# Whole 128-row transposes in place of two 64-row halves in a local-attention decoder

## What is computed

```
x = layernorm(x + ssm(x));  x = layernorm(x + xattn(x, ctx))
for i in range(6):
    x = attn_layer(shift_tokens(x), Wqkv[i], q_scale[i], k_scale[i], Wo[i]) + x
    x = ffn_layer(shift_tokens(x), ...) + x
# attn_layer: qkv = x @ Wqkv, 16 heads of 64; q, k l2-normalised, scaled, rotated (xpos)
#   each window of 32 queries sees the 32 keys before it and its own 32, causal
#   and no further back than 32; softmax(q k^T * 8) v, then @ Wo
# ffn_layer: layer norm, a and gate = xn @ W1 + b1, (a * gelu(gate)) @ W2 + b2
```

## Time and profile before

| what | value |
| --- | --- |
| runs | 2374.88 and 2377.05 us, median 2375.97 |
| profiled execution, span | 2376.2 us |
| PE busy | 2232.7 us (94%) |
| DVE, ACT, POOL busy | 78%, 72%, 69% |
| instructions | 69401 |
| mean granted clock of TensorE | 0.981 |

### The profile page before, as it was taken

One profiled execution on the slowest core, in us unless ns is written; L12 is line 12 of the kernel. 1 busy time (PEld: TensorE's weight loads), 2 busy tenths in 40 slices (PEclk: granted clock), 3 DMA queues, 4 the chain that ended last, 5 costly groups with the idle time before them and its releaser, 6 DMA issues. The chain is left out here.

```text
span 2376.2 us, 69401 instructions
## 1 busy us (share of the span) xinstructions
PE 2232.7 (94%) x26001; PEld 1464.0 (62%) x26001; DVE 1862.1 (78%) x2680; ACT 1703.2 (72%) x3299; POOL 1649.6 (69%) x1553
## 2 busy tenths in 40 slices
PE   5889779999799999999999999999999999999996
PEld 3555446666456666666666666666666666666664
DVE  4899957777678888888888888888888888887884
ACT  5889734544377787787787777787777777777774
POOL 4777832323478778778787787787787787787782
PEclk8999989999899999999999999999999999999997
DMA  2312210000022222222222222222222222222221
GB/s 76 111 59 68 69 51 2 1 1 1 20 63 67 56 76 66 61 71 66 64 68 66 68 65 66 72 61 67 74 58 67 78 54 67 78 53 67 78 53 52
DMA packets 103196, 140.36 MB, mean 59 GB/s; under 512 B 63072, under 2 KB 64096, under 8 KB 102752
## 3 DMA queue, kind: packets, MB, share of 16 engines
q1 hardware_dynamic: 103136, 139.57, 21.7%
HBM read 56.39 MB, written 1.31 MB: 24 GB/s over the span
## 5 line engine op out<-in xcount | busy, mean ns | idle before, releaser
L1799 PE MATMUL f_psA<-f_W,f_xT 128*128 (+1 forms) x1152 | 602.0, 632 | 20.7 <-DVE f_m L1607 12.5
L1607 DVE TENSOR_TENSOR f_m<-f_psA,f_tab 128x1024 f32<-128x1024 f32 x384 | 461.5, 1222 | 120.2 <-ACT f_sq L1468 106.1
L1357 POOL TENSOR_TENSOR f_Pr<-f_Pr,f_rden 128x384 f32<-128x384 f32 x384 | 311.5, 832 | 236.6 <-DVE f_rden L1586 236.6
L1385 POOL TENSOR_TENSOR f_qkr<-f_qkr,f_rn 128x1024 f32<-128x1024 f32 x192 | 361.5, 1904 | 0.2 <-POOL f_rn L1393 0.2
L1799 PEld LDWEIGHTS f_psA<-f_W,f_xT 128*128 128x128 f32 x1152 | 188.9, 190 | 164.5 <-issue 113.4
L1468 ACT ACTIVATE f_sq<-f_psA 128x512 f32<-128x512 f32 x384 | 228.2, 594 | 78.8 <-PE f_psA L1799 76.0
L1770 PEld LDWEIGHTS f_psO<-f_PT,f_V 96*64 96x64 f32 x6144 | 203.5, 138 | 96.4 <-issue 88.5
L1375 POOL TENSOR_TENSOR f_qkr<-f_m 128x512 f32<-128x512 f32 x192 | 244.2, 1272 | 9.1 <-DVE f_m L1607 9.1
L1376 POOL TENSOR_TENSOR f_qkr<-f_m 128x512 f32<-128x512 f32 x192 | 244.2, 1272 | 0.0
L1770 PE MATMUL f_psO<-f_PT,f_V 96*64 96x64 f32 x6144 | 231.9, 227 | 1.6 <-ACT f_PT L1443 1.5
L794 POOL TENSOR_TENSOR x_Es<-x_E 128x512 f32<-128x512 f32 x64 | 81.1, 1267 | 206.1 <-DVE x_E L899 206.1
(11 more groups left out here) (167 smaller groups left out, 4873.5 us busy)
## 6 DMA issues: line engine op xcount, KB each, us to landing
f_V<-f_Vt SPq DMA_DIRECT2D x96, 384.0 KB, 4.2
f_V<-f_Vt SPq DMA_DIRECT2D x96, 256.0 KB, 3.5
f_W<-in_f_W SPq DMA_DIRECT2D x48, 344.0 KB, 3.2
m_Cb<-m_BC_rows SPq DMA_DIRECT2D x64, 256.0 KB, 3.2
f_W<-in_f_W SPq DMA_DIRECT2D x48, 296.5 KB, 4.2
f_V<-f_Vt SPq DMA_DIRECT2D x48, 128.0 KB, 5.3
f_xsA<-xall SPq DMA_DIRECT2D x97, 32.0 KB
f_xsA<-xall SPq DMA_DIRECT2D x97, 31.8 KB
```

The costliest lines, as they stand in the source:

```text
L1357: pool.tensor_tensor(pv, pv, rv.unsqueeze(3).broadcast_to([P, 2, 2, KEYS]), ALU.mult).then_inc(Pr_ready[g][j], 1)
L1385: pool.tensor_tensor(qv, qv, rv.unsqueeze(3).broadcast_to([P, 2, GH, DH]), ALU.mult).then_inc(qkr_ready[g], 1)
L1607: dve.tensor_tensor(m12[:, j, :, half].rearrange("p m (h d) -> p m h d", d=DH), psA[n % 2][:, :].rearrange("p (h d) -> p h d", d=DH).unsqu ...
L1799: pe.matmul(psA[n % 2][:, :], xT[:, t, :], weights(i, W_QKV + n * 512, 512), start=True, stop=True).then_inc(A_full[n_fill], 1)
```

## The change

Transposes take all 128 rows with the whole identity, and the banks hold other things. For the probabilities a bank now holds four heads with both halves (heads 0 to 3 in the first, 4 to 7 in the second), so `P_full` of the first bank is raised after the fourth of eight transposes, and `times_v(g, 0)` waits for both banks. For q and k one bank holds the four blocks of q and the other those of k. The copies of ACT have the same number of elements, with other patterns. There are 8 transposes where 16 were.

```diff
-        PT = sb("f_PT", [KEYS, 2, 8, HQ])
+        PT = sb("f_PT", [KEYS, 2, 4, P])
...
-                    act.activation(PT[:, j, :, :], probs_bank(g, j)[0:KEYS, :].rearrange("p (h q) -> p h q", q=HQ), ACT.Copy).then_inc(P_free[g][j], 1)
+                    act.activation(PT[:, j, :, :], probs_bank(g, j)[0:KEYS, :].rearrange("p (h q) -> p h q", q=P), ACT.Copy).then_inc(P_free[g][j], 1)
...
-                    g, half = n // 2, n % 2
+                    g, a = n // 2, n % 2
                     act.wait_ge(A_full[4 + n], v + 1)
-                    src = psA[g] if half else psP
-                    a = WIN + half * HQ
-                    act.activation(qkT[:, q, :, 4 * g:4 * g + 4, a:a + HQ], src[:, :].rearrange("p (a c q) -> p a c q", a=2, c=4), ACT.Copy).then_inc(A_free[4 + n], 1)
+                    src = psA[g] if a else psP
+                    act.activation(qkT[:, q, a, 4 * g:4 * g + 4, WIN:WIN + P], src[:, :].rearrange("p (c q) -> p c q", c=4), ACT.Copy).then_inc(A_free[4 + n], 1)
...
                     for h in range(8):
-                        for half in range(2):
-                            r = slice(half * HQ, half * HQ + HQ)
-                            ins = pe.transpose(probs_bank(g, half)[0:KEYS, h * HQ:(h + 1) * HQ], Pr[r, g, (h % 2) * 4 + h // 2, :], ident[r, r])
-                            if h == 7:
-                                ins.then_inc(P_full[g][half], 1)
+                        ins = pe.transpose(probs_bank(g, h // 4)[0:KEYS, h % 4 * P:(h % 4 + 1) * P], Pr[:, g, (h % 2) * 4 + h // 2, :], ident[:, :])
+                        if h % 4 == 3:
+                            ins.then_inc(P_full[g][h // 4], 1)
 
                 def times_v(g, half, unit, tile):
-                    pe.wait_ge(P_free[g][half], unit + 1)
+                    if half == 0:
+                        for j in range(2):
+                            pe.wait_ge(P_free[g][j], unit + 1)
...
-                                        V96[:, tile, half, hh_ * DH:(hh_ + 1) * DH], PT[:, half, h, :], start=True, stop=True)
+                                        V96[:, tile, half, hh_ * DH:(hh_ + 1) * DH], PT[:, h // 4, h % 4, half * HQ:(half + 1) * HQ], start=True, stop=True)
...
-                        for half in range(2):
-                            r = slice(half * HQ, half * HQ + HQ)
-                            bank = psA[g] if half else psP
-                            ins = pe.transpose(bank[:, n * HQ:(n + 1) * HQ], qkr[r, q, col:col + P], ident[r, r])
-                            if n == 7:
-                                ins.then_inc(A_full[4 + 2 * g + half], 1)
+                        bank = psA[g] if a else psP
+                        ins = pe.transpose(bank[:, c * P:(c + 1) * P], qkr[:, q, col:col + P], ident[:, :])
+                        if c == 3:
+                            ins.then_inc(A_full[4 + 2 * g + a], 1)
```

## The result

The changed kernel takes 2443.5 us (2441.3 to 2445.7, two runs) against 2376.0 before: a ratio of 1.0283, 95% interval 1.0264 to 1.0302. It is slower by 68 us, where 52 were forecast. A second set of runs, beside the experiments, gave 2445.1 against 2376.2, ratio 1.0284 (1.0268 to 1.0299). Over 48 pairs of slots that is 68 / 48 = 1.41 us a pair, against 1.08 in the forecast.

The account below looks back on a forecast made before the run. PE's instruction order was taken to bound the kernel. Longer transposes and the new times_v wait, less mode switches and covered waits, gave 0.54 us per D or E slot, 1.08 a pair, 52 over 48 pairs: 2428 us, range 2402 to 2460.

Parts of the forecast that it names:

- the rival with the growing wait: Before times_v: square(0) and ACT's second-bank copy move by the whole 0.28 us, both slots lose 0.28 more; 2455 us, chance 0.15.
- PE's order sets the pace: Local-attention layers: PE, 97% busy, sets the pace by its instruction order, apart from short waits.
- the q/k part: Two q/k transpose calls per slot: net +0.09 and +0.20 us in D, +0.05 and +0.20 in E.
- A whole transpose costs its 128 columns: All transpose calls: eight whole take 0.89 us; +0.28 and +0.31 for probabilities, +0.25 twice for q and k, per slot.
- The first rival: All transpose calls: a whole transpose costs no more than a pair, eight some 0.5 us; 2323 us, faster, chance 0.03.
- The mode switches: Around transpose calls: tiling changes that go give back 0.09 us on entering and 0.10 on leaving.
- The copies cost nothing and hardly move: ACT's evacuations: cost 0, bound 0.05 us either way; second bank done 3.00 us (D) or 3.01 (E) behind the first transpose.
- The start of `times_v`: First multiplication with V waits for both banks, starting at 3.05 us; stretch to project(2) costs +0.18 (D) and +0.20 (E).
- the second call for probabilities: Second probability transposes per slot: 0.31 less 0.19 is +0.12 us, less 0.05 in D and 0.03 in E for waits that go.
- The 0.20 of the wait before the scores: E slot, first q/k call: PE's wait for ACT before the scores covers 0.20 of the 0.25 us, leaving 0.05.
- Hidden cost between project(3) and the output projection: That stretch is paced by DVE and POOL, so q/k calls cost nothing; 0.54 us a pair, 2402 us, chance 0.20.

Follow-up runs that it names:

- the banks in their order: Changed kernel, times_v taking heads 0 to 3 for both halves behind the first bank's wait, then heads 4 to 7 behind the second's: 2413.6 us against 2376.2.
- their own run: Kernel before, with only q and k transposed whole and the probabilities left in halves: 2399.1 us against 2378.0, ratio 1.0086.

## Why the prediction was right, and where it was short

The forecast was slower, at 2428 us. The time is 2443.5, inside the range of 2402 to 2460, but 1.5 us above the 2442 at which the forecast's own part of the range ended. The upper part was there for the rival with the growing wait, and that did not happen. So the mechanism was right, and that the range held the time is in part luck. The steps:

*PE's order sets the pace.* Right. The parts add, the q/k part costs what PE's own distances say, and DVE, ACT and POOL have the same busy time as before (1862.1, 1703.3 and 1649.1 us in all) while the kernel got longer.

*A whole transpose costs its 128 columns.* Right, and a little better: 0.87 to 0.89 for eight, where I took 0.89, and 0.93 for the second q/k call, where the sum had 0.94. The first rival, a whole transpose at the price of a pair, is out.

*The mode switches.* Right in size. Projections behind whole transposes are 1.88 us wide for four records (1502.96), where they were 1.98, and 1.95 for the sixteen of the output projection, where they were 2.05. On entering, four such records ahead of the multiplications with V take 1.81 us with the banks in their order (1504.35 to 1506.16) and took 1.91 before. The Trainium skill's rule (TensorEngine Tiling (Array Packing), Key Properties) is that changing the tiling mode drains TensorE; the trace agrees that a change has a price, 0.09 to 0.10 us a side. The loss of the common start outweighs it here.

*The copies cost nothing and hardly move.* Right: 3.02 us behind the first transpose in the D slot against 3.00, and 3.08 in the E slot (1523.59 less 1520.51) against 3.01. So the rival in which the copy grows with PE did not come about, although its price of 2455 is not far off. The time came from another place.

*The start of `times_v`.* This is the term that was too small. I had it start 0.05 us behind ACT, at 3.05 us, a value I assumed and no row showed for the head of a run. It starts 0.34 us behind in a D slot and 0.20 in an E slot, at 3.36 and 3.28. The stretch from the first transpose to project(2) therefore takes 4.72 and 4.36 us (1506.79 less 1502.07, 1524.87 less 1520.51) where I had 4.42 and 4.15. That is 0.51 us a pair, 24 us. The rest of the slots was cheaper than forecast: 1.41 less the stretch's 0.48 and 0.41 leaves 0.52 us a pair, against 0.70, which is 9 us back. 52 + 24 - 9 = 67.

Those 9 us lie about half with the second call for probabilities. Before, W1's products behind project(3) started here:

```profile
1512.33 1.03 PE L1803 MATMUL f_psD<-f_xnT,f_W 128*128 128x256 f32 x4
...
1529.78 1.03 PE L1803 MATMUL f_psD<-f_xnT,f_W 128*128 128x256 f32 x4
```

In the D slot that is 2.60 us behind project(2)'s start at 1509.73, and 2.59 now (1506.79 to 1509.38), where 0.07 more was forecast. In the E slot it is 2.63 (from 1527.15) and 2.69 now (1524.87 to 1527.56), where 0.09 more was forecast. The other half lies with q and k, 0.44 us a pair by their own run, where the sum had 0.54. The 0.20 of the wait before the scores came back as forecast: from the multiplications with V to the scores an E slot takes 1.09 us (1529.39 to 1530.48), and took 1.29.

*Hidden cost between project(3) and the output projection.* The rival of 2402 us is out. It had the q/k calls cost nothing, where the sum had 26 us for them (0.54 a pair), and alone they cost 21.

## What to carry to other kernels

Two 64-row transposes that start together in different halves of the array cost one 64-column stream, some 0.06 us here, so one whole transpose for the pair (0.11) nearly doubles PE's work. The mode switches that go give back only a part. For q and k the longer calls cost a pair of slots 1.04 us (0.23 and 0.29 in each slot); some 0.4 came back with the switches, and 0.2 was a wait that the longer call covered. When data are laid out anew, look at which waits fall together: the late bank's wait moved from the middle of the multiplications to their head and cost nearly as much as the columns. On an in-order engine a wait that ends late belongs behind all other waits and register arithmetic (13 us here), and the work that it gates should start with the part that needs only the early data (31 us here; both gains are on the same wait and do not add).

## What the runs showed of the hardware

How long PE takes to start after a wait ends depends on what stands between the wait and the matmul. In the middle of a run of like multiplications it is hardly seen: before the change the second copy ended at 1507.91 + 0.58 = 1508.49, within the run from 1508.01 to 1509.16, which takes 1.15 us there and 1.09 where nothing is waited for. At the head of the run a semaphore instruction of its own stands between, and it is 0.10 to 0.15 us with that alone, 0.20 with one register instruction behind it and 0.34 with two. A register instruction adds some 0.10 us.

Such a delay need not be told as a wait: the 0.20 of the E slots stood under "issue" and the 0.34 of the D slots under ACT.

The first record of a large matmul behind a switch of tiling takes another 0.10 us: the same two records of project(3) are 1.13 us wide behind 64-row transposes and 1.02 behind whole ones (1508.53).
